# An audio tower on one core: where a quad's experts are chosen, and which PSUM bank holds their logits

## The chip, the cores and the metric

One Trainium2 chip, one of its cores. The metric is device time in microseconds of one execution: the median of three runs, with their lowest and highest beside it. All durations below come from one profiled execution of the kernel.

## What is computed

The input is 32 sequences of 125 rows by 192 channels. Three parts follow each other (the reference, cut):

```python
h = top_k_rows(x, 88 of 125)                     # token choice by a linear score
h = h + attention(layernorm(h))                  # 12 heads of 16, quantized; log2 softmax by integers
h = h + moe(layernorm(h))                        # 16 experts, 4 for each row

# in moe, t = the normalized row
g = t @ gate_w.T + gate_b                        # logits, one for each of 16 experts
vals, idx = top_k(g, 4)
w = softmax(vals) / 4
h1 = swiglu(t @ w1[e] + b1[e])
out = sum over the four of w * (h1 @ w2[e] + b2[e]) * 4
```

The change concerns the logits `g` and the choice of the four experts.

## The kernel before, in words

The 32 sequences are eight *quads* (q = 0 to 7) of four sequences, 352 rows; a quad is held as three tiles of 128 partitions. The attention runs in 24 *slots*, one for each tile (`tile_slots`; slot `st` belongs to quad `st // 3`, and `i = st % 3`), and three more that drain it. Every engine has its own written-out order of work in a function `slot`, and the engines are tied by semaphores alone.

In a slot the vector engine (DVE) does, in this order: the row maxima (`negmx`, L1422), the w pass (`S_w`, L1427), the projection's cast (`pr8`, L1435), in slots with i = 2 the first half of the next quad's values (`quant_v`, L1282), the ratio (L1446), two cheap passes and the mask that ends in `S_p` (L1455), `S_rho` (L1461), `S_pow` (L1464), some small work on rows, `S_e` (L1497), and the sum of `S_e` (L1501). ScalarE (ACT) makes `S_g` from `S_w` (L1011), quantizes the scores of the next tile (L934), and after `S_e` runs a reciprocal root (L1051) and a square (L1057), which the next slot's ratio waits for. GpSimd (POOL) widens int8 to bf16 (L758, L773), makes low halves of weights and rows (L664, L342, L343), and sends routed rows to HBM with indirect DMAs (L765). SyncE (SP) issues transposing loads: of the softmax's result (`pTs<-S_p`, L547, once in a slot), of the normalized rows of a routed quad (`turn_by_load`, L523, in slots with i = 1, ahead of L547), of the attention's rows (L514), and in slots up to 12 it issues the zero fills of `region` (L499).

The router trails the attention. For quad q the gate products are made in slot 3q + 7 (an i = 1 slot): TensorE (PE) does them behind the products of the softmax's result with the values (L1856), and in front of the sixth projection of the next quad (`project_qk(q + 1, 5, ...)`, L1710). In the order that is written out for the shared PSUM bank `pX` (`fill_order`), the logits are one filling among those of the projections: who fills `pX` waits until the filling before has been drained (`xr_drained`), and who drains waits for `xr_filled`. The DVE drains the logits at the head of `top_experts(q)` (L1350), which then picks the four largest (L1353 to L1360, signal `masked`) and subtracts the largest (L1362). `top_experts` is the last thing that the DVE does in slot 3q + 7, behind the sum of `S_e`. In slot 3q + 8 PE counts ranks (`rank_rows`, waits for `masked`) and the DVE finds slots from them (`find_slots`). Quads 0 to 5 have their gate slot within the 24 slots, quad 6 in slot 25, and quad 7's router runs inside the expert steps that follow, on the bank `pO`.

Of the kernel before, what the change touches and what calls it, by code (L numbers as in the profile page):

```python
# [62 lines left out]
def audio_tower(nc, x, tok_w, tok_b, w_qkv, b_qkv, w_proj, b_proj, sw_qkv, sw_proj, s_a1, s_attn,  # L63
                s_a2, s_a3, ffn_scale, gate_w, gate_b, w1, b1, w2, b2, out):
    ctx = ExitStack()
    with ctx:
# [222 lines left out]
        expert_ps = pX[:, 0:3 * E].rearrange("p (i e) -> p i e", i=3)  # L289

        sum_ps = [pS[:, b, 0:C] for b in range(4)]
        rT_last = [pO[:, 0:C * m].bitcast(F16).rearrange("p (k n) -> p k n", k=3) for m in (2, 1)]
# [11 lines left out]
        def y_ps(n):  # L304
# [13 lines left out]
            spread root_ready  # L318
            stage_scaled bias_steps bias_placed stage_high stage_low extra_loaded extra_scaled extra_high extra_low extra_zero
            rows_zeroed route_consts masked gsub_ready exp_ready slots_ready  # L320
            counted tabs_spread table_cols tabs_ready own_ready weights_ready
# [33 lines left out]
        def fill_order():  # L355

            order = []
            for st in range(LAST):
                i, nxt = st % 3, st // 3 + 1 < NQ
                if nxt:  # L360
                    order += [(st, "qk", 1)] if i == 1 else [(st, "v", 0)] if i == 2 else []
                    order += [(st, "qk", 2), (st, "qk", 3)] if i == 1 else []
                if nxt and i != 1:
                    order += [(st, "v", 1)] if i == 2 else []
                if quad_at(st, RANK) is not None:
                    order += [("rank", quad_at(st, RANK))]
                if quad_at(st, TURN) is not None and quad_at(st, TURN) == NQ - 1:
                    order += [("rows", quad_at(st, TURN), m) for m in range(2)]
                if nxt and i == 1:
                    order += [(st, "qk", 4)]  # L370
                if quad_at(st, GATE) is not None:
                    order += [("gate", quad_at(st, GATE))]
                if nxt and i < 2:
                    order += [(st, "qk", 5 * i)]
            return {name: 11 + n for n, name in enumerate(order)}
# [30 lines left out]
        def experts_of(q):  # L406

            return expert_ps if q < NQ - 1 else expert_last

        COLUMNS = ((0, FF, 0), (FF + CA, 2 * FF, FF), (FF, FF + CA, 2 * CA))  # L410
# [27 lines left out]
        def _(sp):  # L438
# [27 lines left out]

            sp.wait_ge(s["extra_zero"], 1)
            gT = gate_w.rearrange("e c -> c e")
# [47 lines left out]
            def turn_by_load(q):  # L516

                sp.wait_ge(s["low2"], 2 * q + 2)
                if q >= 1:
                    sp.wait_ge(s["xr_filled"], fill("gate", q - 1) + 1)  # L520
                    sp.wait_ge(s["ter_copied"], q)
                for i in range(3):
                    sp.dma_start(xTr[:, :, 128 * i:128 * i + 128], rows[q % 3][:, i, 0:2 * C],  # L523
                                 transpose=True).then_inc(s["turned"], 16)
# [29 lines left out]
            turn_x_by_load(1)  # L554
            sp.wait_ge(s["pads_zeroed"], 3)
            for st in range(NT + 1):
# [69 lines left out]
        def _(pool):  # L626
            pool.memset(qkA[:, :], 0.0).then_inc(s["pads_zeroed"], 1)
            pool.memset(qkB[:, :], 0.0).then_inc(s["pads_zeroed"], 1)
            pool.memset(extra[:, :], 0.0).then_inc(s["extra_zero"], 1)

# [218 lines left out]
        def _(act):  # L849
# [99 lines left out]
            def last_rows(q):  # L949
# [5 lines left out]
                if q >= 1:  # L955
                    act.wait_ge(s["xr_filled"], fill("gate", q - 1) + 1)
                act.activation(tEr[0:CB, :], xTr[0:CB, 1, :], ACT.Copy).then_inc(s["ter_copied"], 1)
# [179 lines left out]
        def _(dve):  # L1137
# [208 lines left out]
            def top_experts(q):  # L1346

                logits, chosen = gates[q], masks[:, 3 * q:3 * q + 3, :]
                dve.wait_ge(s["xr_filled"], fill("gate", q) + 1)
                dve.tensor_copy(logits[:, :, :], experts_of(q)).then_inc(s["xr_drained"], 1)  # L1350
                dve.wait_ge(s["xr_drained"], fill("gate", q) + 1)
                for i in range(3):
# [63 lines left out]
            def slot(st, n, q):  # L1416
                i, nxt = st % 3, st // 3 + 1 < NQ
                m = n - 3
                if st < NT:
# [8 lines left out]
                                             negmx[:, :].unsqueeze(2).broadcast_to([128, H, KEEP]), ALU.add,  # L1428
                                             ALU.add).then_inc(s["w_ready"], 1)
                if 3 <= st < NT + 3:  # L1430

# [59 lines left out]
                if st < NT:  # L1491
# [9 lines left out]
                    dve.tensor_reduce(esum[:, :], S_e[:, :, :], AX, ALU.add).then_inc(s["sum_ready"], 1)  # L1501
                if quad_at(st, GATE) is not None:
                    top_experts(quad_at(st, GATE))
# [153 lines left out]
        def _(pe):  # L1657
# [107 lines left out]
            def gate_rows(q):  # L1765
# [4 lines left out]
                else:  # L1770
                    pe.wait_ge(s["tT_drained"], 2)
                pe.wait_ge(s["xr_drained"], fill("gate", q))
                if q == 0:
                    pe.wait_ge(s["extra_low"], 3)
                    pe.wait_ge(s["route_consts"], ROUTE_CONSTS)
                for i in range(3):
                    cols = slice(128 * i, 128 * i + 128)
                    for n, (lhs, kind) in enumerate(((xTr[:, 0, cols], 0), (xTr[:, 0, cols], 1), (xTr[:, 2, cols], 0),
                                                     (xTr[:, 1, cols], 2), (tEr[:, cols], 3))):
                        ins = pe.matmul(experts_of(q)[:, i, :], lhs, gws[:, kind, :], start=n == 0, stop=n == 4)  # L1780
                ins.then_inc(s["xr_filled"], 1)

# [203 lines left out]
```

## Time and profile before

| what | us |
|---|---|
| median of 3 runs | 656.92 (655.81 to 658.57) |
| the profiled execution | 655.91 |
| its span, first to last instruction | 654.2 |
| DVE busy | 535.4 (82%) |
| ACT busy | 443.6 (68%) |
| POOL busy | 403.3 (62%) |
| PE busy | 360.0 (55%) |

The span is from the first instruction to the last; 1.7 us of the profiled execution lie outside it. The attention's slots run from 74 us to about 425 us of the span, the expert steps follow. A line of the timeline gives an instruction's start in us from the start of the span, its duration, engine, source line and operands, and in brackets how long the engine sat idle in front of it and what ended that.

### The profile page before, as it was taken

What the parts mean: (1) busy time and instruction counts of PE and PEld (TensorE: products, weight loads), DVE (VectorE), ACT (ScalarE), POOL (GpSimd) and SP (SyncE); (2) the same over time, 40 slices, a digit from 0 to 9 for tenths busy, and PEclk for the clock granted to TensorE, in tenths of its full rate; (3) what the DMA queues carried; (4) which work ended last, traced back from release to release, by engine and by line L of the source; (5) the groups of instructions that cost most, each with busy time, mean ns of one, the idle gap of its engine ahead of it and who ended that gap; (6) DMA issues with size and microseconds to landing.
All of it is one profiled execution on the core that took longest, in us unless ns stands there. A gap on an engine that the chain in (4) does not pass through costs nothing.

```text
span 654.2 us, 13296 instructions
## 1 busy us (share of the span) xinstructions
PE 360.0 (55%) x3593; PEld 238.3 (36%) x3593; DVE 535.4 (82%) x1380; ACT 443.6 (68%) x782; POOL 403.3 (62%) x450
## 2 busy tenths in 40 slices
PE   0498254063451633534536221268979999998264
PEld 0144112021130311311313111256757677776163
DVE  3688699679898897799997989669769988999576
ACT  0045657478777677677686874376878899999753
POOL 9783433431546486587785885577777877777500
PEclk9999555565555555555555555578989999999569
DMA  8645997787959969743422332467466668663098
GB/s 193 69 70 171 369 279 148 256 252 207 314 125 333 226 205 323 155 106 83 111 58 61 95 72 65 104 142 149 116 136 147 123 139 146 129 140 60 20 397 295
DMA packets 191977, 107.76 MB, mean 165 GB/s; under 512 B 137747, under 2 KB 186012, under 8 KB 191907
## 3 DMA queue, kind: packets, MB, share of 16 engines
q1 hardware_dynamic: 181634, 89.22, 55.4%
q0 software_dynamic: 10272, 17.70, 9.3%
q8 instruction: 33, 0.54, 0.3%
q14 instruction: 38, 0.30, 0.1%
HBM read 23.61 MB, written 60.67 MB: 129 GB/s over the span
## 4 chain that ended last, share of the span: by engine, by line
DVE 27%; issue 18%; DMA 13%; SPq 13%; ACT 11%; PE 9%; POOL 7%; DVEq 1%; POOLq 0%; ACTq 0%
POOL expert_rows L836 6%; DMA pTs<-S_p 6%; SPq L523 5%; DVE S_e L1497 4%; DVE negmx L1422 3%; SPq L611 2%; DMA w2s<-expert_rows 2%; DMA arena<-in_x_dram 2%; PE pS L1666 2%; SPq L514 2%; PE pS L1668 2%; DMA expert_rows<-stage,dest 2%; DMA bias_rows_hl<-bias_hl 2%; DVE S_w L1427 2%; DVE arena L1628 1%
## 5 line engine op out<-in xcount | busy, mean ns | idle before, releaser
L836 POOL DMA_INDIRECT expert_rows<-stage,dest x118 | 122.8, 1040 | 36.1 <-issue 31.1
L765 POOL DMA_INDIRECT region<-rows,slots x60 | 73.8, 1230 | 23.5 <-issue 16.3
L758 POOL CAST arena<-arena 128x384 bf16<-128x384 int8 x42 | 26.5, 632 | 70.7 <-ACT arena L926 70.0
L765 POOL DMA_INDIRECT region<-arena,slots x36 | 46.4, 1288 | 18.4 <-issue 11.2
L1843 PE MATMUL pP<-WpT,oq 128*128 128x192 bf16 x72 | 15.9, 359 | 74.8 <-ACT oq L1025 70.1
L926 ACT ACTIVATE arena<-pX,qkB,qkA 128x384 int8<-128x384 f32 x43 | 28.5, 662 | 41.7 <-PE pX L1710 41.7
L1710 PE MATMUL pX<-arena,WA 128*128 128x384 f16 x86 | 35.0, 509 | 39.3 <-ACT arena L926 28.2
L664 POOL TENSOR_TENSOR w1s<-stage,w1s 128x768 f16<-128x768 f32 (+1 forms) x16 | 33.9, 2116 | 32.0 <-ACT w2s L912 31.4
L1497 DVE SCALAR_TENSOR_TENSOR S_e<-S_sq,kf,S_pow 128x1056 f32<-128x1056 f32 x24 | 38.6, 1609 | 16.5 <-ACT S_sq L1039 16.4
L1856 PE MATMUL pO<-pTs,vq 88*32 88x96 bf16 (+1 forms) x576 | 12.5, 238 | 71.1 <-DMA pTs<-S_p 71.0
L1011 ACT ACTIVATE S_g<-S_w,kf 128x1056 int16<-128x1056 uint16 x24 | 30.3, 1264 | 27.8 <-DVE S_w L1427 27.8
L1051 ACT ACTIVATE S_sq<-S_e,kf 128x1056 f32<-128x1056 f32 x24 | 28.1, 1172 | 26.0 <-DVE S_e L1497 26.0
L1628 DVE TENSOR_SCALAR arena<-pS 128x512 f32<-128x512 f32 x59 | 40.4, 685 | 3.0 <-PE pS L1923 2.9
L1446 DVE SCALAR_TENSOR_TENSOR S_ratio<-esum,S_sq 128x1056 uint16<-128x1056 f32 x24 | 31.0, 1291 | 10.2 <-ACT S_sq L1057 10.1
L1856 PEld LDWEIGHTS pO<-pTs,vq 88*32 88x32 bf16 x576 | 8.7, 118 | 80.3 <-DMA pTs<-S_p 80.0
L1843 PEld LDWEIGHTS pP<-WpT,oq 128*128 128x128 bf16 x72 | 7.8, 130 | 79.4 <-ACT oq L1025 72.4
L1737 PE MATMUL pS<-arena 32*96 32x88 bf16 (+1 forms) x576 | 32.9, 277 | 5.5 <-ACT S_u L934 4.7
L1923 PE MATMUL pS<-arena,w1s 128*128 128x256 f16 x224 | 34.0, 282 | 0.0
L1422 DVE TENSOR_REDUCE negmx<-S_u 128x12 f32<-128x1056 int8 x24 | 29.9, 1244 | 4.7 <-ACT S_u L934 4.7
L1461 DVE SCALAR_TENSOR_TENSOR S_rho<-S_g,kf,S_w 128x1056 int16<-128x1056 int16 x24 | 32.3, 1347 | 1.3 <-ACT S_g L1011 1.3
L1427 DVE SCALAR_TENSOR_TENSOR S_w<-S_u,kf,negmx 128x1056 uint16<-128x1056 int8 x24 | 32.4, 1350 | 0.8
L1923 PE MATMUL pS<-tEb,w1s 128*128 128x256 f16 x118 | 32.9, 279 | 0.0
(428 smaller groups left out, 1413.6 us busy)
## 6 DMA issues: line engine op xcount, KB each, us to landing
region<-zrow SPq DMA_DIRECT2D x11, 3200.0 KB, 12.2
w1s<-expert_rows SPq DMA_DIRECT2D x16, 384.0 KB, 7.9
stage<-in_L_ffn_w_dram SPq DMA_DIRECT2D x16, 192.0 KB, 2.9
stage<-in_L_ffn_w_dram SPq DMA_DIRECT2D x32, 96.0 KB, 2.9
w2s<-expert_rows SPq DMA_DIRECT2D x8, 384.0 KB, 11.8
arena<-in_x_dram SPq DMA_DIRECT2D x4, 672.0 KB
expert_rows<-stage,dest POOLq DMA_INDIRECT x118
out_dram<-xsel SPq DMA_DIRECT2D x8, 198.0 KB
```

Of the source, the lines that this page charges most:

```text
L523: sp.dma_start(xTr[:, :, 128 * i:128 * i + 128], rows[q % 3][:, i, 0:2 * C], transpose=True).then_inc(s["turned"], 16)
L664: pool.tensor_tensor(ws[rows, kind + 1, two, :], st[rows, :, at:at + width], ws[rows, kind, two, :], ALU.subtract).then_inc(s["stage_low"], 1)
L765: pool.indirect_dma_start(region_rows, bass.IndirectOffsetOnAxis(ap=slots[q % 3][:, i, m:m + 1], axis=0), rows[q % 3][:, i, :].bitcast(I16 ...
L836: pool.indirect_dma_start(y_dram, bass.IndirectOffsetOnAxis(ap=dest[(st - 7) % 8][:, j:j + 1], axis=0), ysb[b][:, j, :], None, bounds_chec ...
L1422: dve.tensor_reduce(negmx[:, :], S_u[:, :, :], AX, ALU.max, negate=True).then_inc(s["max_ready"], 1)
L1427: dve.scalar_tensor_tensor(S_w[:, :, :], S_u[:, :, :], k(K_C), negmx[:, :].unsqueeze(2).broadcast_to([128, H, KEEP]), ALU.add, ALU.add).th ...
L1461: dve.scalar_tensor_tensor(S_rho[:, :, :], S_g[:, :, :], k(K_X), S_w[:, :, :], ALU.mult, ALU.subtract).then_inc(s["rho_ready"], 1)
L1497: dve.scalar_tensor_tensor(S_e[:, :, :], S_sq[:, :, :], k(K_KK), S_pow[:, :, :].bitcast(BF16), ALU.add, ALU.mult).then_inc(s["e_ready"], 1)
L1628: dve.tensor_scalar(lin[r], hidLC[r], -6.0 * XS * WS, 8.0 * XS * WS, ALU.max, ALU.min).then_inc(s["l_done"], 1)
L1710: ins = pe.matmul(bank[:, 0:384], W[:, 128 * c:128 * c + 128], xT[:, kind, :], start=n == 0, stop=n == 2)
L1737: ins = pe.matmul(pS[rows, j, KEEP * c:KEEP * c + width], qT[r][blk, c, at:at + m], keys, start=True, stop=True)
L1923: ins = pe.matmul(dst, w1s[:, kind, bass.ds(k_, 1), 128 * window:128 * window + 128].rearrange("p o f -> p (o f)"), rhs, start=n == 0, sto ...
```

## The change

In the slots, `top_experts(q)` moves from the end of the gate slot 3q + 7 to the next slot, 3q + 8, behind the w pass and in front of `pr8`. That is so for the quads 0 to 5; quad 6 keeps its place at the end of slot 25, and quad 7 its place in the expert steps. The logits of the quads 0 to 6 get a PSUM bank of their own, `pP[:, 0, :]`, and a semaphore of their own, `logits_ready`; they are no longer a filling of `pX`, so PE's sixth projection no longer waits for the DVE's copy of the logits. PE waits for `masked` of the quad before instead of a drained `pX`. The waits of SP and ACT for the gate products are renamed. The semaphore `extra_zero` is merged into `pads_zeroed`.

```diff
+        logits_ps = pP[:, 0, :].bitcast(F32)[:, 0:3 * E].rearrange("p (i e) -> p i e", i=3)
...
-                if quad_at(st, GATE) is not None:
-                    order += [("gate", quad_at(st, GATE))]
...
+        def logits_of(q):
+            return logits_ps if q < NQ - 1 else expert_last
...
# SP, turn_by_load, and ACT, last_rows
-                    sp.wait_ge(s["xr_filled"], fill("gate", q - 1) + 1)
+                    sp.wait_ge(s["logits_ready"], q)
...
# DVE, top_experts
-                dve.wait_ge(s["xr_filled"], fill("gate", q) + 1)
-                dve.tensor_copy(logits[:, :, :], experts_of(q)).then_inc(s["xr_drained"], 1)
-                dve.wait_ge(s["xr_drained"], fill("gate", q) + 1)
+                dve.wait_ge(s["logits_ready"], q + 1)
+                link(dve.tensor_copy(logits[:, :, :], logits_of(q)))
...
# DVE, slot, behind the w pass
+                if st < NT and quad_at(st - 1, GATE) is not None:
+                    top_experts(quad_at(st - 1, GATE))
...
# DVE, slot, at its end
-                if quad_at(st, GATE) is not None:
+                if st >= NT and quad_at(st, GATE) is not None:
                     top_experts(quad_at(st, GATE))
...
# PE, gate_rows
-                pe.wait_ge(s["xr_drained"], fill("gate", q))
+                if q >= 1:
+                    pe.wait_ge(s["masked"], q)
...
-                        ins = pe.matmul(experts_of(q)[:, i, :], lhs, gws[:, kind, :], start=n == 0, stop=n == 4)
-                ins.then_inc(s["xr_filled"], 1)
+                        ins = pe.matmul(logits_of(q)[:, i, :], lhs, gws[:, kind, :], start=n == 0, stop=n == 4)
+                ins.then_inc(s["logits_ready"], 1)
```

## Rows read from the trace of the kernel before

**Rows 1.** The page, part 1: busy us, share of the span, instructions.
```profile
PE 360.0 (55%) x3593; PEld 238.3 (36%) x3593; DVE 535.4 (82%) x1380; ACT 443.6 (68%) x782; POOL 403.3 (62%) x450
```
**Rows 2.** The view of waits: engine, line, releaser: us in total, times, longest.
```profile
DVE arena L1350 <- PE pX L1780: 9.0, 7, 2.1
```
**Rows 3.** Timeline of the DVE: the copies of the logits, quads 0 to 5.
```profile
182.30 0.21 DVE L1350 COPY arena<-pX 128x48 f32<-128x48 f32 x1 [0.38 <-PE pX L1780]
...
223.80 0.21 DVE L1350 COPY arena<-pX 128x48 f32<-128x48 f32 x1 [1.13 <-PE pX L1780]
...
268.96 0.21 DVE L1350 COPY arena<-pX 128x48 f32<-128x48 f32 x1 [1.47 <-PE pX L1780]
...
311.09 0.21 DVE L1350 COPY arena<-pX 128x48 f32<-128x48 f32 x1 [1.78 <-PE pX L1780]
...
353.42 0.21 DVE L1350 COPY arena<-pX 128x48 f32<-128x48 f32 x1 [2.11 <-PE pX L1780]
...
392.79 0.21 DVE L1350 COPY arena<-pX 128x48 f32<-128x48 f32 x1 [1.52 <-PE pX L1780]
```
**Rows 4.** The chain that ended last, around slot 13: start us, us, what.
```profile
255.43 1.95 SPq L523
...
262.63 5.22 DMA pTs<-S_p
...
267.90 0.52 PE pO L1856 x24
...
268.43 0.51 PE pX L1780 x15
```
**Rows 5.** Timeline of the DVE, end of slot 13 and start of slot 14.
```profile
266.24 1.25 DVE L1501 TENSOR_REDUCE esum<-S_e 128x12 f32<-128x1056 f32 x1
...
270.58 1.25 DVE L1422 TENSOR_REDUCE negmx<-S_u 128x12 f32<-128x1056 int8 x1
271.86 1.32 DVE L1427 SCALAR_TENSOR_TENSOR S_w<-S_u,kf,negmx 128x1056 uint16<-128x1056 int8 x1
273.09 0.35 DVE L1435 TENSOR_TENSOR pr<-pP,pA 128x192 int8<-128x192 f32 x1
273.36 0.54 DVE L1282 TENSOR_TENSOR arena<-pX,vA 96x384 int8<-96x384 f32 x1
273.82 1.25 DVE L1446 SCALAR_TENSOR_TENSOR S_ratio<-esum,S_sq 128x1056 uint16<-128x1056 f32 x1
```
**Rows 6.** Timeline of PE, the same stretch: the sixth projection, the values' last matmul.
```profile
269.23 0.82 PE L1710 MATMUL pX<-arena,WA 128*128 128x384 f16 x2 [0.30 <-DVE arena L1350]
...
272.28 0.36 PE L1723 MATMUL pX<-tabi,one_of 128*96 128x192 bf16 x1
```
**Rows 7.** Timeline of ACT, the same stretch.
```profile
270.98 1.07 ACT L1057 ACTIVATE S_sq<-S_sq 128x1056 f32<-128x1056 f32 x1
```
**Rows 8.** Timeline of POOL, slots 14 and 15.
```profile
271.25 0.51 POOL L758 CAST arena<-arena 128x384 bf16<-128x384 int8 x1 [3.48 <-ACT arena L926]
272.08 1.96 POOL L765 DMA_INDIRECT region<-rows,slots  x1 [0.33 <-issue]
...
279.99 1.00 POOL L765 DMA_INDIRECT region<-rows,slots  x1 [0.16 <-issue]
...
292.50 1.66 POOL L664 TENSOR_TENSOR w1s<-stage,w1s 128x768 f16<-128x768 f32 x1
```
**Rows 9.** Timeline of the DVE: two `S_e` passes, slots 13 and 15.
```profile
264.88 1.32 DVE L1497 SCALAR_TENSOR_TENSOR S_e<-S_sq,kf,S_pow 128x1056 f32<-128x1056 f32 x1 [1.54 <-ACT S_sq L1039]
...
293.11 2.18 DVE L1497 SCALAR_TENSOR_TENSOR S_e<-S_sq,kf,S_pow 128x1056 f32<-128x1056 f32 x1 [1.07 <-ACT S_sq L1039]
```
**Rows 10.** Timeline of SP's queue in slot 11.
```profile
234.69 3.78 SPq L514 DMA_TRANSPOSE arena<-arena  x3
238.52 0.58 SPq L499 DMA_DIRECT2D region<-zrow  x1
```
**Rows 11.** Timeline of PE in slot 12.
```profile
254.27 0.52 PE L1856 MATMUL pO<-pTs,vq 88*32 88x96 bf16 x24 [8.65 <-DMA pTs<-S_p]
```

More of the change, by code:

```diff
@@ L318, in audio_tower @@
             spread root_ready
-            stage_scaled bias_steps bias_placed stage_high stage_low extra_loaded extra_scaled extra_high extra_low extra_zero
-            rows_zeroed route_consts masked gsub_ready exp_ready slots_ready
+            stage_scaled bias_steps bias_placed stage_high stage_low extra_loaded extra_scaled extra_high extra_low
+            rows_zeroed route_consts logits_ready masked gsub_ready exp_ready slots_ready
             counted tabs_spread table_cols tabs_ready own_ready weights_ready
@@ L465, in _ @@
                           src[0:2 * C].rearrange("(c j d) -> j d c", j=4, d=DH)[j])
-            sp.wait_ge(s["extra_zero"], 1)
+            sp.wait_ge(s["pads_zeroed"], 3)
             gT = gate_w.rearrange("e c -> c e")
@@ L554, in _ @@
             turn_x_by_load(1)
-            sp.wait_ge(s["pads_zeroed"], 3)
+            sp.wait_ge(s["pads_zeroed"], 4)
             for st in range(NT + 1):
@@ L628, in _ @@
             pool.memset(qkB[:, :], 0.0).then_inc(s["pads_zeroed"], 1)
-            pool.memset(extra[:, :], 0.0).then_inc(s["extra_zero"], 1)
+            pool.memset(extra[:, :], 0.0).then_inc(s["pads_zeroed"], 1)
             for t in (idf, idh, idb):
@@ L955, in last_rows @@
                 if q >= 1:
-                    act.wait_ge(s["xr_filled"], fill("gate", q - 1) + 1)
+                    act.wait_ge(s["logits_ready"], q)
                 act.activation(tEr[0:CB, :], xTr[0:CB, 1, :], ACT.Copy).then_inc(s["ter_copied"], 1)
```

## The prediction

> **What bounds the kernel now.** I read the page first, for which engine is full, then the waits, for what the DVE lacks when it is idle, then the chain that ended last around one gate slot, and at last the timelines of that stretch for the order and the slack of each engine. Times of the working are those of quad 2 (gate slot 13, next slot 14) unless I say otherwise.
>
> The DVE is the fullest engine [rows 1], and in the slots it seldom rests. One of its rests belongs to the part that is changed: the copy of the logits is waited for seven times, 9.0 us in all [rows 2]. The six within the slots stand one by one: 0.38, 1.13, 1.47, 1.78, 2.11 and 1.52 us, 8.4 together [rows 3]; 0.6 are left for quad 6. The reader is to see two things. The idle time stands directly in front of the copy, so nothing else held the DVE up. And it comes every third slot, grows to 2.1 us and has no other cause than PE being late.
>
> The chain says why PE is late [rows 4]. SP first issues the transposing loads of the routed rows, from 255.43 on, and only at 262.63 that of the softmax's result; it lands 5.22 us later, PE multiplies it (267.90), and the gate products come behind that (268.43). The logits are there at 268.96. The DVE had ended the sum of `S_e` at 267.49 [rows 5] and stood still. So in a gate slot the path that sets the end leaves the DVE, goes over SP, DMA and PE, and comes back with the logits.
>
> **The change, part by part.** *The move.* `top_experts` costs the DVE 1.62 us, from the copy's start to the next `negmx` (268.96 to 270.58) [rows 3, 5]. Nothing of that goes away. But in the new order `negmx` and the w pass come first. They need nothing from PE's gate products. `negmx` takes 1.28 us and the w pass 1.23, start to start, 2.51 together [rows 5]. A pass that waits for nothing starts a little before the end of the one in front, as `pr8` does 0.09 us before the w pass ends (273.09 against 273.18) [rows 5]. So I let `negmx` start 0.08 us before the sum's end, at 267.41, where the copy started at 268.96: 1.55 us, 0.08 more than the idle time in the row. With 2.51 us of other work in front of it, `top_experts` arrives at 269.92, behind the logits (268.96). For the worst quad the logits come 2.11 + 0.08 = 2.19 us behind that point, still less than 2.51. So all six waits at the copy go, quad 6's 0.6 stays. That is 8.4 + 6 x 0.08 = 8.9 us off the DVE's own order, the largest gain that this can have.
>
> *What is late next.* In slots with i = 2 and a next quad (quads 0 to 4), the DVE soon needs PE again, for the first half of the values (`quant_v`, L1282). PE makes these behind the sixth projection, which is behind the gate products. The values' last matmul starts at 272.28 and takes 0.36 us [rows 6], so `quant_v` can start at about 272.68, which is 3.72 us behind the logits. It did start at 273.36, 4.40 behind [rows 5]. The slack is 0.68 us.
>
> *The bank and the signal.* PE's sixth projection sat idle 0.30 us for the DVE's copy [rows 6]. With a bank of its own for the logits it follows at once. ACT's quantizing and PE's values behind it come 0.30 us earlier too. The slack at `quant_v` grows to 0.68 + 0.30 = 0.98 us. That is the cap of what quads 1 to 4 can gain; what is over it comes back as a wait at L1282. Gains: quad 0: 0.38 + 0.08 = 0.46. Quad 1: 1.21, capped to 0.98. Quads 2, 3 and 4: 1.55, 1.86 and 2.19, each capped to 0.98. Quad 5 has no next quad and no `quant_v`: 1.60. Sum: 0.46 + 4 x 0.98 + 1.60 = 5.98 us.
>
> *Other things that the DVE meets in slot 14.* The ratio needs ACT's square, over at 272.05 [rows 7]; the ratio comes no earlier than 272.84 (273.82 less 0.98) [rows 5], so that costs nothing. ACT's `S_g` waits for the w pass, which is now over some 3 us earlier; ACT can start it when its square is done. That shortens ACT's side and costs nothing. `masked` comes later for PE's ranks in slots with i = 2, but the ranks stand behind the second half of the values, which comes behind `quant_v`, and this now stands behind `top_experts`: no cost. In slot 23 (quad 5) PE has no values, and its ranks wait for `masked` with the projection behind them; the projection waits for ACT longer than that. No cost, and 1.6 us if that cover were gone.
>
> *Renamed waits, the merged semaphore.* SP's and ACT's waits for the gate products fire at the same matmul as before, and the three memsets on POOL are in the same order. PE's wait for `masked` of the quad before is over since two slots. Nothing.
>
> *Whether POOL keeps pace.* The zero fills and the weights' low halves hang on POOL. A POOL instruction and a DVE pass stretch each other: `S_e` took 1.32 us where POOL was free and 2.18 where `w1s` (292.50, 1.66 us) was running when it started [rows 8, 9]. The send at 272.08 took 1.96 us beside the w pass, where another took 1.00 [rows 8]. In the new order the w pass is over before that send starts, so POOL gains about 1 us there, as much as the DVE gains, and both go on together. I take the gain to be kept. The other end: POOL's cast of the sixth projection (271.25) starts only 0.30 us earlier, and if everything behind it shifts by that alone, then `S_e` runs into `w1s` and loses what it had gained. Then quads 1 to 4 are worth 0.30 each, and quad 0 as well: 5 x 0.30 + 1.60 = 3.1 us. I take the first, since the stretched send is seen in this very place.
>
> The Trainium skill says of this (SBUF — State Buffer, section "SBUF: two separate sides") that the port pair which VectorE and GpSimd share is an exclusive lock, held for a whole instruction, and that an operation of VectorE with two SBUF inputs must wait for it. The trace agrees: 293.11 to 295.29 is the rest of `w1s` (to 294.16) and a pass of 1.1 to 1.3 us. By that rule the moved instructions, which had POOL idle beside them, now meet the cast and may wait up to its 0.51 us; in front of a wait at `quant_v` that is free, and without one it would make the sum 5.98 - 0.5 = 5.5 us.
>
> *The zero fills.* In slots 8 to 12 the transposing load of the softmax's result waits for DMA, not for the DVE: PE waited 8.65 us for it [rows 11], behind the fill issued at 238.52, which SP issues behind the transposes of 234.69 [rows 10]. These wait for POOL's low halves. So what quads 0 and 1 gain goes on only if POOL comes earlier too. With POOL's shift as taken above it does; with 0.30 each, these two are worth 0.6 in place of 1.44.
>
> **Sum.** The profiled execution took 655.91 us and would take 655.91 - 5.98 = 649.9. The median of the runs is 1.0 above it: 656.92 - 5.98 = 650.9 us, 0.9% less.
>
> **The rivals.** *A: the gain is kept as worked out.* 650.9, with a range of its own from 649 to 653.5. Chance 0.58.
>
> *B: POOL or the fills take it back.* Behind each gate slot only the 0.30 us of the bank are left, or not even this in quads 0 to 4; quad 5's 1.60 stays. That is 1.6 to 3.1 us: 653.8 to 655.3. For it speaks that POOL, once it has begun in slot 14, idles only 0.16 to 0.33 us in front of its instructions [rows 8], so it has little slack to give; against it the stretched send. The lower part is within 0.5%. Chance 0.24.
>
> *C: no cap at `quant_v`.* If PE's values come earlier than I read from their last matmul, or ACT's earlier `S_g` also takes waits off `S_e` (those in rows 9 were 1.54 and 1.07 us), the gain is the whole 8.9 us: 648.0. Against it: the values' place in PE's queue is fixed behind the gate products. Chance 0.1.
>
> *D: slower.* The mutual stretching of DVE and POOL turns against the new order: the ratio and the two passes behind it slide into POOL's three sends of slot 14, which had the w pass and the ratio beside them. One such collision costs the DVE up to one send, 1.0 us [rows 8]. If it happens twice in each of five quads, 10 us are lost and 6 won: 656.9 + 4 = 661. It decides when the collisions cost more than 0.98 us for each quad. A late logit would do it as well, as the DVE then blocks with ratio and softmax behind it, but this needs more than 2.51 us, and 2.19 is the worst. Chance 0.08.
>
> **How the numbers follow.** A measurement of this kernel can tell a change of about 0.5%, 3.3 us, from none. Faster by more than that: A nearly whole (0.56), C (0.1) and a little of B (0.04): 0.70. Within: the rest of B and some of D: 0.25. Slower: 0.05. The range of eight in ten goes from C's edge, 648.3, to B's upper edge, 655.5.
>
> **What the changed profile would show.** The idle time at L1350 falls from 9.0 to about 0.6 us, quad 6's. The 0.30 us in front of the sixth projection go. New idle time stands in front of L1282 in slots 11, 14, 17 and 20, about 0.2, 0.6, 0.9 and 1.2 us. `S_g` starts without waiting for the w pass in slots 8, 11, 14, 17, 20. DVE busy stays near 535. Three slots together, from 16 to 19, take about 1 us less. Wrong it would be if L1350 is idle again in its new place, if idle time at L1446 or L1497 grows by as much as L1350 lost, or if `S_e`, `S_w` or the ratio get longer beside POOL.

## The result, and the profile after

The changed kernel takes 648.8 us (median of 4 runs, 648.06 to 649.23); the kernel before takes 656.95 (655.81 to 658.57). The difference of the medians is 8.1 us. The ratio on record is 0.9885, with a 95% interval from 0.9847 to 0.9923: 7.6 us less, and by the interval 5 to 10. (Here and below a ratio on record can differ a little from the quotient of the two medians.) The forecast was 650.9, 6.0 us less.

The page first. The DVE does the same work as in [rows 1], 0.3 us more of it, in a span that is 7.9 us shorter: what went was idle time.

```profile
PE 358.6 (55%) x3593; PEld 237.5 (37%) x3593; DVE 535.7 (83%) x1380; ACT 444.2 (69%) x782; POOL 398.9 (62%) x450
```

The view of waits (engine, line, releaser: us in total, times, longest). The copy of the logits is now L1353; of the 9.0 us of [rows 2] it keeps quad 6's 0.6. At the first half of the values (L1285) there are two waits that the kernel before did not have, 1.5 us together; one is put down to "issue".

```profile
DVE arena L1353 <- PE pP L1785: 0.6, 1, 0.6
...
DVE arena L1285 <- issue: 1.0, 1, 1.0
...
DVE arena L1285 <- PE pX L1727: 0.5, 1, 0.5
```

Timeline of the DVE, the copies of quads 0 to 5 (start us, us, engine, line, what). None has a bracket behind it: no idle time, where [rows 3] have 0.38 to 2.11 us each.

```profile
182.61 0.20 DVE L1353 COPY arena<-pP 128x48 f32<-128x48 f32 x1
...
223.06 0.20 DVE L1353 COPY arena<-pP 128x48 f32<-128x48 f32 x1
...
266.85 0.20 DVE L1353 COPY arena<-pP 128x48 f32<-128x48 f32 x1
...
307.18 0.20 DVE L1353 COPY arena<-pP 128x48 f32<-128x48 f32 x1
...
348.39 0.20 DVE L1353 COPY arena<-pP 128x48 f32<-128x48 f32 x1
...
386.89 0.20 DVE L1353 COPY arena<-pP 128x48 f32<-128x48 f32 x1
```

Timeline of the DVE around quad 2's choice, the stretch of [rows 5]. `negmx` starts 0.08 us before the sum ends (264.42), the copy 2.51 us behind it, and `quant_v` has no idle time in front.

```profile
263.17 1.25 DVE L1505 TENSOR_REDUCE esum<-S_e 128x12 f32<-128x1056 f32 x1
264.34 1.24 DVE L1424 TENSOR_REDUCE negmx<-S_u 128x12 f32<-128x1056 int8 x1
265.62 1.32 DVE L1429 SCALAR_TENSOR_TENSOR S_w<-S_u,kf,negmx 128x1056 uint16<-128x1056 int8 x1
...
268.55 0.35 DVE L1439 TENSOR_TENSOR pr<-pP,pA 128x192 int8<-128x192 f32 x1
268.81 0.54 DVE L1285 TENSOR_TENSOR arena<-pX,vA 96x384 int8<-96x384 f32 x1
269.28 1.25 DVE L1450 SCALAR_TENSOR_TENSOR S_ratio<-esum,S_sq 128x1056 uint16<-128x1056 f32 x1
```

Timeline of PE there. The sixth projection (L1714) starts at 265.18, inside the last gate product, where [rows 6] have 0.30 us of idle time. The values for `quant_v` end at 268.58, 3.26 us behind the end of the gate products (265.32).

```profile
265.15 0.17 PE L1785 MATMUL pP<-gws,tEr 128*128 128x16 f16 x1
265.18 0.80 PE L1714 MATMUL pX<-arena,WA 128*128 128x384 f16 x2
...
268.21 0.37 PE L1727 MATMUL pX<-tabi,one_of 128*96 128x192 bf16 x1
```

Timeline of POOL there, and in slot 15. The first send of slot 14 takes 0.99 us, not the 1.96 of [rows 8]; the two behind it, beside the ratio and `S_rho`, take 2.08 and 2.04, where they took 1.58 and 2.03 in the kernel before. `w1s` starts at 287.95, and `S_e` of that slot at 288.56: 0.61 us behind it, the very distance of [rows 8, 9] (292.50 and 293.11). POOL has come forward by as much as the DVE (4.55 us at both).

```profile
267.17 0.51 POOL L761 CAST arena<-arena 128x384 bf16<-128x384 int8 x1 [2.60 <-ACT arena L929]
268.01 0.99 POOL L768 DMA_INDIRECT region<-rows,slots  x1 [0.33 <-issue]
269.30 2.08 POOL L768 DMA_INDIRECT region<-rows,slots  x1 [0.30 <-issue]
271.68 2.04 POOL L768 DMA_INDIRECT region<-rows,slots  x1 [0.30 <-issue]
...
287.95 4.29 POOL L667 TENSOR_TENSOR w1s<-stage,w1s 128x768 f16<-128x768 f32 x2
```

Timeline of the DVE in slots 15, 17 and 20: that `S_e`, and the two waits in front of `quant_v`. The line of L1364 belongs to slot 20; it took 0.20 us elsewhere and 0.51 here.

```profile
288.56 2.18 DVE L1501 SCALAR_TENSOR_TENSOR S_e<-S_sq,kf,S_pow 128x1056 f32<-128x1056 f32 x1 [1.07 <-ACT S_sq L1042]
...
310.13 0.55 DVE L1285 TENSOR_TENSOR arena<-pX,vA 96x384 int8<-96x384 f32 x1 [0.99 <-issue]
...
349.88 0.51 DVE L1364 TENSOR_TENSOR arena<-arena,best 128x48 f32<-128x48 f32 x1
...
351.20 0.55 DVE L1285 TENSOR_TENSOR arena<-pX,vA 96x384 int8<-96x384 f32 x1 [0.55 <-PE pX L1727]
```

Timeline of POOL, the cast beside which L1364 ran.

```profile
349.75 0.57 POOL L761 CAST arena<-arena 128x384 bf16<-128x384 int8 x1 [4.72 <-ACT arena L929]
```

**Where the time went, slot by slot.** I count a slot from one `negmx` of the DVE to the next, and the gate slot of a quad together with the one behind it, so that the moved 1.62 us stay inside the pair. Quad 5's choice leaves its pair only by the slot's edge, so 1.62 are taken off there.

| quad | idle at the copy before | pair before | pair after | gain | forecast |
|---|---|---|---|---|---|
| 0 | 0.38 | 28.24 | 27.88 | 0.36 | 0.46 |
| 1 | 1.13 | 30.57 | 29.45 | 1.12 | 0.98 |
| 2 | 1.47 | 32.61 | 31.15 | 1.46 | 0.98 |
| 3 | 1.78 | 29.57 | 28.77 | 0.80 | 0.98 |
| 4 | 2.11 | 28.66 | 27.67 | 0.99 | 0.98 |
| 5 | 1.52 | 14.56 (one slot) | 11.34 + 1.62 | 1.60 | 1.60 |

That is 6.3 us, and slot 21 is 0.46 shorter: 6.8 from slot 7 on. The 0.46 is `S_e`, 1.74 us in place of 2.20. It can't be credited to the change: in the second profile of the kernel before, unaltered, `S_e` of slot 21 takes 1.74 as well. The profiled spans differ by 7.9 us; another 1.6 lie in front of slot 7, in code that the change does not touch. Slot 7 starts at 166.3 us in this profile, at 167.9 in the one before, and anywhere from 167.3 to 169.6 in those of the experiments, in an order that has nothing to do with their edits: I take the 1.6 as spread of single executions. About 0.5 us was given back behind the slots.

### The profile page after: what moved, and what is told of

Same layout as the page of the kernel before. It is cut to its first block, busy times and chain, and to the rows that moved or that the text cites. A ratio compares the mean times of both kernels' runs of the same rounds, so it can differ in the third digit from the quotient of the medians.

```text
span 646.3 us, 13296 instructions
## 1 busy us (share of the span) xinstructions
PE 358.6 (55%) x3593; PEld 237.5 (37%) x3593; DVE 535.7 (83%) x1380; ACT 444.2 (69%) x782; POOL 398.9 (62%) x450
## 4 chain that ended last, share of the span: by engine, by line
DVE 27%; issue 17%; ACT 15%; DMA 12%; SPq 6%; PE 4%; POOL 3%; DVEq 1%; POOLq 0%; ACTq 0%
DMA pTs<-S_p 6%; DVE S_e L1501 4%; DVE negmx L1424 3%; POOL expert_rows L839 3%; ACT stage L1104 2%; DVE S_ratio L1450 2%; DMA expert_rows<-stage,dest 2%; SPq L614 2%; ACT tEb L1112 2%; DVE S_w L1429 2%; DMA w2s<-expert_rows 2%; ACT S_sq L1042 2%; DVE S_rho L1465 2%; DVE arena L1632 2%; DMA bias_rows_hl<-bias_hl 2%
## 5 line engine op out<-in xcount | busy, mean ns | idle before, releaser
L768 POOL DMA_INDIRECT region<-arena,slots x36 | 44.4, 1233 | 18.3 <-issue 11.2
L1714 PE MATMUL pX<-arena,WA 128*128 128x384 f16 x86 | 34.8, 508 | 37.5 <-ACT arena L929 28.8
L1501 DVE SCALAR_TENSOR_TENSOR S_e<-S_sq,kf,S_pow 128x1056 f32<-128x1056 f32 x24 | 38.2, 1591 | 16.6 <-ACT S_sq L1042 16.4
L1014 ACT ACTIVATE S_g<-S_w,kf 128x1056 int16<-128x1056 uint16 x24 | 30.3, 1263 | 18.8 <-DVE S_w L1429 18.8
```

The lines of the kernel that those rows point to most:

```text
L768: pool.indirect_dma_start(region_rows, bass.IndirectOffsetOnAxis(ap=slots[q % 3][:, i, m:m + 1], axis=0), rows[q % 3][:, i, :].bitcast(I16 ...
L1501: dve.scalar_tensor_tensor(S_e[:, :, :], S_sq[:, :, :], k(K_KK), S_pow[:, :, :].bitcast(BF16), ALU.add, ALU.mult).then_inc(s["e_ready"], 1)
L1714: ins = pe.matmul(bank[:, 0:384], W[:, 128 * c:128 * c + 128], xT[:, kind, :], start=n == 0, stop=n == 2)
```

## The experiments

Two theories stood against each other on what the parts are worth. Theory 1 is that of the prediction: the time comes from the idle time at the copy, and the bank only keeps PE from waiting. Theory 2: the bank and its signal give a good part alone, as PE's queue no longer waits for the DVE. The first four kernels ran on one chip, beside the kernel before (656.99 us median of 29 runs, 653.95 to 659.55). The others ran on two further chips, on which every version that ran took longer; each time is compared with the kernel before on its own chip.

**The bank alone.** From the changed kernel, the choice is put back at the end of the gate slot.

```diff
-                if st < NT and quad_at(st - 1, GATE) is not None:
-                    top_experts(quad_at(st - 1, GATE))
...
-                if st >= NT and quad_at(st, GATE) is not None:
+                if quad_at(st, GATE) is not None:
                     top_experts(quad_at(st, GATE))
```

> The logits' own bank and signal, with the choice of experts left at the end of the gate slot. Theory 1 (the gain is the DVE's idle time in front of the copy, and the bank only widens the cap at quant_v): the six waits of 0.4 to 2.1 us at the copy stay, the 0.30 us in front of PE's sixth projection go, and nobody waits for them: 656 to 657 us, within 0.5 us of the kernel before. Theory 2 (the shared bank's order was what held the slot: the chain PE, ACT, POOL behind the sixth projection set the pace): 653 us or less.

Measured: 654.49 us (653.09 to 655.93), ratio 0.9972 [0.9953, 0.999], 1.8 us less. The idle time at the copies stays (10.0 us over seven copies). So the bank is worth something alone, against theory 1, but only about a quarter of the whole. The trace shows the larger part of it, first in POOL's timeline and then in the DVE's, both of slot 15:

```profile
289.02 1.10 POOL L768 DMA_INDIRECT region<-rows,slots  x1 [0.30 <-issue]
293.39 4.25 POOL L667 TENSOR_TENSOR w1s<-stage,w1s 128x768 f16<-128x768 f32 x2 [3.27 <-ACT w2s L915]
```

```profile
294.40 1.73 DVE L1499 SCALAR_TENSOR_TENSOR S_e<-S_sq,kf,S_pow 128x1056 f32<-128x1056 f32 x1 [1.07 <-ACT S_sq L1042]
```

POOL had ended its sends 3.27 us early and began `w1s` as soon as ACT's half was there, 1.01 us ahead of `S_e` and not 0.61. So `S_e` met less of it: 1.73 us in place of 2.18 to 2.20, in each of slots 12, 15, 18 and 21. Four times 0.46 is 1.8 us, of the 2.2 that the DVE saves from slot 7 to slot 22. It is a balance and not the only difference: in slots 11, 14 and 17 `S_e` falls from 1.88 us to 1.32, but `S_rho`, 1.30 before, meets POOL's low halves of the rows and takes 2.47. Timeline of the DVE, slot 14 (POOL's L343 and L344 run from 277.09 to 278.66):

```profile
277.31 2.47 DVE L1463 SCALAR_TENSOR_TENSOR S_rho<-S_g,kf,S_w 128x1056 int16<-128x1056 int16 x1
```

In the changed kernel none of this is part of the gain: in slots 12, 15 and 18 `S_e` takes 2.18 to 2.19 us again, in slots 11, 14 and 17 it takes 1.88 to 1.89, and `S_rho` 1.30.

**The move alone.** In the kernel before, only the place of the choice is changed; the logits stay a filling of `pX`.

```diff
+                if st < NT and quad_at(st - 1, GATE) is not None:
+                    top_experts(quad_at(st - 1, GATE))
...
-                if quad_at(st, GATE) is not None:
+                if st >= NT and quad_at(st, GATE) is not None:
                     top_experts(quad_at(st, GATE))
```

> The kernel before with the choice of experts moved behind the w pass, and the logits still one filling of pX, so that PE's sixth projection waits for the moved copy. Theory 1 (cap): the copy comes 2.51 us behind the sum instead of 0.46 to 2.19, PE's values come 3.72 us behind the copy, and quant_v, which had 4.40, waits for them. Quads 0 to 4 change by +1.4, +0.6, +0.3, 0.0 and -0.4 us, quad 5 by -1.6: together +0.3, so 656.5 to 658 us; idle time of 8 to 10 us appears at quant_v. Theory 3 (only the place matters, the bank is decoration): 649 to 651 us.

Measured: 656.51 us (654.82 to 658.0), ratio 0.9994 [0.9977, 1.001]: nothing that can be told from the kernel before, as its Theory 1 had it. The idle time at the copy is gone and stands again at `quant_v`, 8.7 us over five slots. Timeline of PE, slot 14, then of the DVE: the projection waits 1.76 us for the copy, and the DVE 1.75 us for the values behind it.

```profile
271.79 0.82 PE L1712 MATMUL pX<-arena,WA 128*128 128x384 f16 x2 [1.76 <-DVE arena L1350]
```

```profile
271.53 0.20 DVE L1350 COPY arena<-pX 128x48 f32<-128x48 f32 x1
...
275.24 0.55 DVE L1282 TENSOR_TENSOR arena<-pX,vA 96x384 int8<-96x384 f32 x1 [1.75 <-PE pX L1725]
```

So the move needs the bank. The bank alone is worth 1.8 us, the move alone nothing that can be measured, and both together 7.6 (8.1 by the medians).

**Quad 5 alone moved.** From the changed kernel, only quad 5's choice goes to the next slot.

```diff
-                if st < NT and quad_at(st - 1, GATE) is not None:
+                if st < NT and quad_at(st - 1, GATE) == 5:
                     top_experts(quad_at(st - 1, GATE))
...
-                if st >= NT and quad_at(st, GATE) is not None:
+                if quad_at(st, GATE) not in (None, 5):
                     top_experts(quad_at(st, GATE))
```

> The changed kernel, but only quad 5's choice moves; quads 0 to 4 keep the end of the gate slot. Theory 1: quad 5 is worth its whole wait, 1.6 us: 655.3 us, and the waits of quads 0 to 4 (0.4, 1.1, 1.5, 1.8, 2.1) are back. A rival (some of the measured 8.1 us has nothing to do with the waits and came from slots 0 to 7, where the changed profile is already 1.6 us ahead): 653 to 654 us, with slots 0 to 7 ahead of the kernel before as well.

Measured: 654.02 us (652.19 to 655.24), ratio 0.9952 [0.9935, 0.9969]. That is 0.5 us under the bank alone by the medians and 1.3 by the ratios; the two intervals overlap, so the times show no effect of the move beyond the bank's. The 654.0 is the rival's figure (653 to 654), but its sign is missing: slot 7 starts at 168.1 us, not ahead of the kernel before (167.9). The 655.3 of Theory 1 left out what the bank alone is worth. In the trace the term is exact: slot 22 takes 11.34 us and not 14.56, which less the moved 1.62 is 1.60. The other five copies still wait (0.65 to 2.47 us).

**The values later.** From the changed kernel, the first half of the values is taken behind `S_p`, not in front of the ratio.

```diff
-                if nxt and i == 2:
-                    quant_v(q + 1, 0, fill(st, "v", 0))
... (behind S_p, ahead of the wait for S_g)
+                if nxt and i == 2:
+                    quant_v(q + 1, 0, fill(st, "v", 0))
```

> The changed kernel with the first half of quant_v put behind the softmax mask (S_p) instead of in front of the ratio. Theory 1: the two waits that the changed profile shows at quant_v (0.99 us in slot 17, 0.55 in slot 20) are the cap, and go: 1.5 us less than the changed kernel, 647 to 647.5 us. Rival: PE's second half of the values, the ranks and the projection stand behind the drained first half, come 2 us later and make the next pass wait: no gain or 1 to 2 us more, 649 to 651 us.

Measured: 648.94 us (647.44 to 650.65), ratio 0.9878 [0.9851, 0.9905]; the change has 0.9885. The waits at the first half are gone, 0.22 us in each of four slots come back at the second half, and from slot 7 to slot 22 the DVE needs 205.7 us in place of 206.8. The 1.5 us that were expected are 1.1 in the slots, and in the whole time they can't be seen. Nor are the 1.1 the two waits alone: `S_e` falls in the same profile from 2.18 or 2.19 us to 1.73 in slots 12, 15 and 18, 1.4 us together, so the edit also moved POOL and the DVE against each other.

**The two kernels again, on a slower chip.** Both unchanged.

> The changed kernel once more, unaltered. The slot-by-slot reckoning of its first profile finds 6.8 us behind slot 7 and 1.6 us in front of it, where the code did nothing new. If those 1.6 are the spread of one execution, the median over more runs is 649 to 650.5 us (6.5 to 8 us under the kernel before); if they belong to the change, 648 to 649 and slots 0 to 7 are ahead in this profile too.

> The kernel before against itself: ratio 1.000 within 0.2%. Its second profile shows how much slots 0 to 7, and each wait at the copy, move from one execution to the next: I expect 1 to 2 us at the start of slot 7 and under 0.3 us for the sum of the six waits.

Measured: the kernel before takes 741.83 us on this chip (736.01 to 747.51, 27 runs). Before again: 742.60, ratio 1.0012 [0.9982, 1.0042]. After again: 734.92, ratio 0.9923 [0.9897, 0.9948], 5.7 us less by the ratio and 6.9 by the medians. From slot 7 to 22 the DVE takes 211.1 and 207.1 us (212.0 and 206.8 on the first chip), so the slots keep their length to within 1 us. Slot 7 starts at 167.7 us in the changed kernel and at 168.9 in the kernel before, ahead once more. But the profiles whose code is the same up to slot 7 show no order: from slot 0 to slot 7 the kernel before takes 93.6 and 93.6 us and the move alone 91.9; the changed kernel takes 92.5, 92.2 and 92.6 (in the order of its profiles), the bank alone 93.2, quad 5 alone 92.3, and the change with the table step moved 93.4. The 1.6 us of the first pair are therefore spread.

The kernel before, again, missed one expectation, and it bears on the forecast. The waits at the copy were to differ by under 0.3 us in their sum. The first five are 0.55, 1.19, 1.40, 0.42 and 1.95 us, 5.5 together, where [rows 3] have 6.9 for the same five; quad 3's alone went from 1.78 to 0.42. (The sixth is 7.32, and has another cause; see below.) Timeline of the DVE, quad 3's copy in this profile:

```profile
311.40 0.21 DVE L1350 COPY arena<-pX 128x48 f32<-128x48 f32 x1 [0.42 <-PE pX L1780]
```

So the term on which the forecast rests differs by 1.4 us between two executions of one kernel.

**Quad 6's order.** From the changed kernel, the table step of slot 25 goes ahead of quad 6's choice, to cover its 0.6 us.

```diff
+                if st == NT + 1:
+                    step_table(0)
                 if st >= NT and quad_at(st, GATE) is not None:
                     top_experts(quad_at(st, GATE))
                 if st == NT:
                     step_blocks(0)
-                if st == NT + 1:
-                    step_table(0)
```

> The changed kernel with the step table of slot 25 made in front of quad 6's choice of experts, whose wait (0.6 us) and 1.6 us of work then no longer stand before the table that SP's first loads wait for. Theory 1: SP's loads are what the expert steps start behind: 1 to 2 us less than the changed kernel. Rival: the steps start behind ACT's work on quad 7's rows, which follows from the same DVE work in either order: within 0.3 us of it.

Measured: 734.09 us (728.97 to 739.21), ratio 0.9899 [0.9867, 0.9931]. Quad 6's 0.6 us of idle time are gone. The interval of this ratio and that of the change on this chip overlap; inconclusive.

**POOL's weights first.** From the changed kernel, POOL makes the low halves of the weights ahead of its sends in slots with i = 0.

```diff
+                if i == 0 and st < NT:
+                    low_pair(q)
                 if st <= NT:
                     send((3, 0, 3)[i] if st < NT else 2)
-                if i == 0 and st < NT:
-                    low_pair(q)
```

> The changed kernel with POOL's low halves of the weights put in front of the three sends in slots with i = 0. Theory (S_e is stretched from 1.32 to 2.19 us in slots 12, 15, 18 because w1s has begun some 0.6 us before it, and a w1s begun 0.5 us earlier leaves that much less): S_e 1.7 us in these slots, 1.4 us less than the changed kernel. Rival: the sends, now behind the weights, make POOL's casts of the projections late, the scores of the next quad wait for them, and it is 1 to 3 us slower.

Measured: 733.36 us (730.7 to 737.45), ratio 0.990 [0.9864, 0.9936]. `S_e` takes 1.73 to 1.74 us in slots 12, 15, 18 and 21 as expected (in slot 21 the change on this chip has that already), and slots 7 to 22 take 204.3 us, 2.8 less than in the change on this chip. The whole time does not show it. The next runs ask where it goes.

**The same edit on the kernel before; both edits on the changed kernel; the change a third time.** The edits are those of the two diffs above (POOL's weights first; the values later and POOL's weights first). This third chip has the kernel before at 739.88 us (734.5 to 743.37, 25 runs).

> The kernel before, with one edit: in slots with i = 0 POOL makes the low halves of the weights (w1s, w2s) ahead of its three sends and not behind them. In the kernel with the bank alone S_e took 1.73 us in slots 12, 15, 18 and 21 where the kernel before has 2.19, because POOL had ended its sends early and w1s began as soon as ACT's half was there, 1.0 us ahead of S_e and not 0.6. Theory 1 (this alignment is what the bank alone gained, and it is kept): S_e 1.73 in the four slots, ratio about 0.997 (1.8 us less), and slots 0 to 23 about 1.8 us shorter. Theory 2 (the sends that now come later take it back from the w pass and the ratio of the next slot): S_e 1.73 all the same, S_w 1.6 to 1.7 in the slots behind, time and slots unchanged, ratio 1.000.

> The kernel after, with two edits that alone could not be told from it: the first half of the values is taken behind S_p and not in front of the ratio, and POOL makes the weights' low halves ahead of the sends in slots with i = 0. Theory 1 (the two losses that are left, the wait at the values and S_e beside w1s, are independent): no wait at the first half of the values, S_e 1.73 in slots 12, 15, 18 and 21, slots 0 to 23 some 1.5 to 2 us shorter than in the kernel after, ratio to the kernel before about 0.986. Theory 2 (each is taken back by POOL's sends that slide beside S_w or S_rho): slots 0 to 23 as long as in the kernel after, within 0.5 us, ratio as that of the kernel after in this call.

> The kernel after unchanged, so that it stands beside the other two on one chip with five rounds. Both theories: ratio 0.986 to 0.991 to the kernel before (6 to 9 us less; the first measurement gave 0.9885, the second, on a slower chip, 0.9923), slots 0 to 23 in 310.6 us as in both profiles so far if these slots do not depend on the chip.

| kernel | us | ratio | slots 7 to 22 | idle at quad 5's copy |
|---|---|---|---|---|
| before, on the second chip | 742.60 | 1.0012 [0.9982, 1.0042] | 211.1 | 7.32 |
| before, weights first | 740.13 | 1.0008 [0.998, 1.0037] | 209.6 | 8.55 |
| the change, third time | 733.61 | 0.9905 [0.9873, 0.9938] | 206.9 | 4.68 |
| the change, both edits | 733.83 | 0.992 [0.9888, 0.9953] | 204.2 | 7.52 |

With the weights first the slots are shorter in both kernels, by 1.5 us and 2.7 us (the 1.5 is a difference between two chips, and the 2.7 belong to both edits; the weights alone gave 2.8 on the second chip, so the values later added nothing that shows). Behind the slots the gain is gone: quad 5's copy comes at the same distance from slot 7 as without the edits. Here is quad 5's copy of the logits in the kernel with both edits, then in the change (timelines of the DVE, slot 23), and PE's last gate product for it in the former:

```profile
393.60 0.21 DVE L1353 COPY arena<-pP 128x48 f32<-128x48 f32 x1 [7.52 <-remote]
```

```profile
393.44 0.21 DVE L1353 COPY arena<-pP 128x48 f32<-128x48 f32 x1 [4.68 <-remote]
```

```profile
384.88 0.17 PE L1785 MATMUL pP<-gws,tEr 128*128 128x16 f16 x1
```

The logits are there at 385.05, and the DVE starts the copy 8.5 us later, at the same time as in the change, though it had come to it 2.7 us earlier. The profile names no engine of the core as the releaser ("remote"). What it waits for the profile does not show, but what was won in the slots is lost at this place: 2.84 us more idle time against 2.7 won. From the start of slot 7 to this copy it is 225.5 to 225.7 us in the change and in the change with the weights first, on either chip, and 229.8 and 229.5 in the kernel before without and with them. So the end of this wait does not depend on when the DVE comes to it, yet it is not free of the program either: the change brought it forward by 4 us, the weights first did not. Theory 2 of these two runs was right in the total and wrong in the cause: the slots are shorter, and `S_w` is longer in slots 11, 17 and 20 of the kernel with both edits (1.65 to 1.69 us), but in no slot of the kernel before with the weights first. Whether the two edits would help on the first chip, where the copy has no such wait, was not measured together; the values later alone did not show there.

## Why the prediction was right, point by point

**The idle time at the copy.** Right, to the row: seven waits of 9.0 us became one of 0.6. `negmx` started 0.08 us ahead of the sum's end as taken, and the logits came at most 2.1 us behind the sum, less than the 2.51 us of other work. ACT's `S_g` no longer waits for the w pass in the five slots that were named (8, 11, 14, 17 and 20), and in all it waits 18.8 us where it was 27.8; as foreseen, `S_e`'s own waits for ACT did not fall by it (16.4 us in both kernels). The profile pair shows the place, the move alone shows that the place by itself is worth nothing, and quad 5 alone shows its term exact at 1.60 us in the trace. The size is less sure than the row made it look: in the second profile of the kernel before five of the six waits sum to 1.4 us less, and the forecast read them from one execution.

**The bank.** The prediction gave the bank only its 0.30 us. That without it the sixth projection would wait for the moved copy, and the whole gain with it, is not in the prediction; it was expected first for the move alone, which shows it (8.7 us at `quant_v`). Here the sum had its mis-sized term, the cap. I took the values to be ready 3.72 - 0.30 = 3.42 us behind the logits. From the end of the gate products to the end of the values it is 3.72 us in the kernel before and 3.25 in the changed kernel, in all five quads: 0.47 less. The 0.30 of the row were only the idle time; without it the sixth projection also overlaps the last gate product by 0.14 (265.18 against 265.32). With the sum's end as the zero point the DVE reaches `quant_v` at 4.39 us. So a quad pays when its logits come more than 4.39 - 3.25 = 1.14 us behind the sum.

**How late the logits are.** The forecast took each quad's lateness from one profile of the kernel before. It moves, with the change and without it. The gate products end behind the sum of `S_e` by

| quad | 0 | 1 | 2 | 3 | 4 | 5 |
|---|---|---|---|---|---|---|
| before | 0.35 | 1.09 | 1.43 | 1.75 | 2.07 | 1.48 |
| after | 0.66 | 1.20 | 0.90 | 2.09 | 1.95 | 1.50 |
| before, again | 0.51 | 1.16 | 1.36 | 0.38 | 1.91 | 1.51 |
| after, third time | 0.24 | 1.22 | 0.96 | 1.74 | 1.95 | 1.53 |

With the first profile after, quad 1 is at the limit and quad 2 under it, so their gain is not capped (1.12 and 1.46 us, where 0.98 each was forecast). Quad 3 pays 2.09 - 1.14 = 0.95, and its wait is 0.99. Quad 4 pays 0.81: 0.55 of wait and 0.31 in front of it, where L1364 ran beside POOL's cast. The forecast had 0.2, 0.6, 0.9 and 1.2 us of new waits in slots 11, 14, 17 and 20; there were 0, 0, 0.99 and 0.55. Summed, with the 0.31, the caps cost 1.9 us and not 2.9. So the sum would have been 8.9 - 1.9 = 7.0; the six rows of the table above show 6.3. The 0.7 between are small losses, some 0.1 us in each of quads 0 to 3 and 0.3 in quad 4 (0.08 in front of the wait, where a pass that waits can't start ahead of the end of the last, and 0.25 in front of and in `S_e` of slot 20).

**What was luck.** That quad 4 gained 0.99 us where 0.98 was forecast is luck: with the waits as they were it would have kept 2.19 - 0.86 = 1.33 us, and 0.34 of other losses brought that down. In the total, too, misses of opposite sign meet: quads 1 and 2 gained 0.14 and 0.48 more than forecast, quads 0 and 3 gained 0.10 and 0.18 less. The measured 648.8 lies just under the range that rival A gave itself (649 to 653.5) and nearer to C's 648.0 than to A's 650.9; it is the traces, and not the time, that speak for A.

**The rest of the 8.1.** The slots account for 6.8 in one pair of profiles, 0.46 of them the `S_e` of slot 21 that the change did not make. On the slower chips the difference from slot 7 to 22 is 4.0 to 4.2 us, where the first pair has 5.2, and the rest comes at quad 5's copy with its long wait: up to the `pr8` of slot 23, behind quad 5's choice, the change is 6.6 to 6.8 us ahead, as it is in the first pair (6.6). The three measurements of the whole time give 7.6, 5.7 and 7.0 us by their ratios. The interval of the first, 5 to 10, holds 6.8 and the forecast's 6.0 alike. What is over 6.8 in the first is not explained by anything in the traces.

**POOL keeps pace.** Right in the outcome, and half right in the reason. The first send ran in 0.99 us as foreseen, but the next two grew from 1.58 and 2.03 us to 2.08 and 2.04, so the three saved 0.46 and not about 1 (0.67 in quads 1, 3 and 4). The rest of what quad 2 gained came in front of them: POOL's cast of the sixth projection starts 2.75 us behind the DVE's sum and no longer 3.76, about half of it because the logits were 0.53 us less late, the other half because PE no longer waits for the DVE. From the end of the sends on, POOL and DVE stand to each other as before, to 0.01 us (`w1s` and `S_e`, 0.61 apart in both). So rival B, that POOL or the fills take it back, fell: quad 0 and quad 1 kept 0.36 and 1.12 of at most 0.46 and 1.21, fills and all.

**The moved instructions beside the cast.** The Trainium skill (SBUF — State Buffer, section "SBUF: two separate sides") says that VectorE and GpSimd share a port pair under an exclusive lock, and that VectorE's operations with two SBUF inputs need it. The trace agrees in kind: L1364, which has two such inputs, took 0.51 us with POOL's cast from 349.75 to 350.32 beside it, and 0.20 without. It ended 0.07 us behind the cast, a little sooner than a full wait and its own 0.20 would have it. As the prediction said of this rule, it costs nothing there, since 0.31 us less stand as a wait behind it.

**Rival C, no cap at all,** fell for quads 3 and 4 and held for 1 and 2. It named values that come earlier than read, which was right by 0.17 us (3.25 against 3.42), and `S_e`'s waits, which did not move (16.4 us in both kernels). **Rival D** fell: the full passes of slots 8 to 20 have the durations of before to 0.05 us, but for the w pass of slot 8, which is shorter (1.52 to 1.32), though the sends stand beside others of them. That such a meeting could cost 1.2 us is seen in the bank alone.

**A step that was left out.** The bank alone was not costed, but for the cap. It is worth 1.8 us alone, in the trace mainly four `S_e` passes of 1.73 us in place of 2.19. The gain does not add to that of the move, which brings POOL and DVE back to the old distance.

## What to carry to other kernels

When an engine waits for a result that another makes, look at what of its own next work does not need that result, and put it in front: the gain is the idle time, up to the slack of the next thing it needs from that same queue. A buffer shared with the other queue undoes the move, since the wait then only changes its place; the move alone brought nothing that could be measured, the buffer alone 1.8 us, both together about 7. Read that slack as the distance between two ends of work, not from the idle time of one row, and read the lateness of each instance from more than one execution before summing caps: quad 3's was 1.75 us in one profile of the kernel before and 0.38 in the other.

## What was not expected of the hardware

The same kernel takes 656.9 us on one chip, 741.8 on a second and 739.9 on a third. The attention's slots take the same time on the first two (212.0 and 211.1 us from slot 7 to 22, at a granted clock of 0.51 of full speed from 74 to 385 us on both); slot 22 starts at 379.9 and at 380.0 us, so all of the 85 us lie behind it. From 385 us to the end the granted clock is 0.85 on the first chip and 0.81 on the second, and PE is busy for 212 us there in place of 190; the DVE and ACT are busy hardly longer (218 and 200 us in place of 215 and 198). The view of waits for the kernel before on the second chip shows them as idle time whose releaser the profile calls "remote", which the first chip's does not have at all:

```profile
ACT arena L1091 <- remote: 25.7, 6, 12.3
...
ACT stage L1086 <- remote: 22.4, 10, 5.3
DVE arena L1628 <- remote: 21.2, 5, 6.1
...
DVE cnt L1518 <- remote: 16.4, 2, 8.7
```

What these waits are was not found. For the reader they matter in one way: a gain in front of such a wait may vanish, as that of the weights first did here, so the times of kernels were compared only on one chip.
